# Numbers per token spread over partitions by DMAs through DRAM, rows scaled on GpSimd, and a new order of work

## What is computed

```python
def rmsnorm(x, gamma):
    n = jnp.linalg.norm(x, axis=-1, keepdims=True)
    return x / jnp.maximum(n, 1e-12) * SCALE * gamma
xn = rmsnorm(x, norm_gamma)                      # x here: the layer-normed rows, xn2 in the kernel
sn = rmsnorm(slot_embeds, slot_norm_gamma)       # 8 experts x 64 slots
logits = jnp.einsum('bnd,esd->bnes', xn, sn)
dispatch = jax.nn.softmax(logits, axis=1)        # over the tokens
combine = jax.nn.softmax(logits.reshape(b, n, e * s), axis=-1)   # over the slots, for each token
slots = jnp.einsum('bnd,bnes->besd', xn, dispatch)
h = gelu(jnp.einsum('besd,edh->besh', slots, w1) + b1)
eo = jnp.einsum('besh,ehd->besd', h, w2) + b2
out = jnp.einsum('bmd,bnm->bnd', eo, combine)
```

## Time and profile before

| | before |
|---|---|
| median of 3 runs | 1098.13 us (1097.9 to 1098.71) |
| profiled execution, its own time | 1098.24 us |
| its span (first to last instruction) | 1096.4 us, mean TensorE clock 0.992 of full speed |
| TensorE busy | 1062.8 us (97%) |
| VectorE busy | 960.2 us (88%) |
| ScalarE busy | 773.0 us (71%) |
| GpSimd busy | 606.9 us (55%) |
| share of the chain that ended last | PE 90%, DVE 6% |

### The profile page before, as it was taken

How to read it: one execution, slowest core, us unless ns; L and a number is a source line. 1 busy time by engine, 2 the same in 40 slices (tenths; PEclk the granted TensorE clock), 3 DMA queues, 4 the chain that set the end, 5 groups by cost and what they waited for, 6 DMA issues and landing times.

```text
span 1096.4 us, 27975 instructions
## 1 busy us (share of the span) xinstructions
PE 1062.8 (97%) x10436; PEld 832.9 (76%) x10436; DVE 960.2 (88%) x2074; ACT 773.0 (71%) x1450; POOL 606.9 (55%) x619
## 2 busy tenths in 40 slices
...
DMA packets 18468, 16.97 MB, mean 15 GB/s; under 512 B 800, under 2 KB 17440, under 8 KB 18080
## 3 DMA queue, kind: packets, MB, share of 16 engines
...
## 4 chain that ended last, share of the span: by engine, by line
PE 90%; DVE 6%; issue 1%; ACT 1%; POOL 0%; POOLq 0%; DVEq 0%; ACTq 0%
PE bank L1008 12%; PE bank L959 11%; PE bank L969 10%; PE bank_s L990 7%; PE bank L950 5%; PE bank L979 5%; PE bank L920 5%; PE bank L913 5%; PE bank L1035 3%; DVE ret L661 3%; PE bank L908 3%; PE bank L823 3%; PE bank L874 3%; PE bank L1018 3%; PE bank_s L993 2%; PE bank L854 2%
## 5 line engine op out<-in xcount | busy, mean ns | idle before, releaser
L329 POOL TENSOR_TENSOR ret_abs<-ret_abs 128x512 f32<-128x512 f32 x128 | 168.7, 1318 | 238.2 <-ACT ret_abs L485 238.2
L661 DVE TENSOR_TENSOR ret<-bank_s,k_sb 128x1536 f32<-128x1536 f32 x128 | 223.9, 1749 | 23.7 <-PE bank L1008 14.8
L334 POOL TENSOR_TENSOR urs<-uvar,mhalf 128x16 f32<-128x16 f32 x64 | 185.3, 2903 | 91.8 <-DVE uvar L677 91.8
L485 ACT ACTIVATE ret_abs<-ret 128x1536 f32<-128x1536 f32 x128 | 189.6, 1481 | 8.8 <-DVE ret L661 8.8
L959 PE MATMUL bank<-slotsT,w_sb 128*128 128x128 f32 x1024 | 140.9, 281 | 0.3 <-DVE hact L726 0.3
L969 PEld LDWEIGHTS bank<-w_sb,hact 128*128 128x128 f32 x1024 | 125.5, 192 | 14.7 <-issue 13.9
L969 PE MATMUL bank<-w_sb,hact 128*128 128x128 f32 x1024 | 134.1, 277 | 0.0
L959 PEld LDWEIGHTS bank<-slotsT,w_sb 128*128 128x128 f32 x1024 | 124.3, 192 | 10.3 <-issue 7.4
L340 POOL TENSOR_SCALAR dT<-dT,drec 128x256 f32<-128x256 f32 x128 | 83.4, 665 | 48.6 <-DVE drec L721 48.4
L1008 PE MATMUL bank<-ret,vrow 128*32 128x256 f32 (+1 forms) x2048 | 108.6, 329 | 0.3 <-DVE hact L726 0.2
L990 PE MATMUL bank_s<-qT,km 32*128 32x256 f32 x1024 | 91.4, 426 | 5.0 <-DVE ret L661 5.0
...
## 6 DMA issues: line engine op xcount, KB each, us to landing
x_sb<-x SPq DMA_DIRECT2D x16, 256.0 KB, 2.8
...
out<-attn SPq DMA_DIRECT2D x16, 256.0 KB, 2.3
...
slot_sb<-slot_rows SPq DMA_DIRECT2D x1, 256.0 KB, 3.5
```

Source lines behind the costliest of these rows:

```text
L329: pool.tensor_tensor(both[:, :, P:SEQ], both[:, :, P:SEQ], both[:, :, SEQ:3 * P], ALU.add)\
L334: pool.tensor_tensor(urs[:, j], uvar[:, j], mhalf[:], ALU.pow).then_inc(ready["urs"].sem, 1)
L485: act.activation(ret_abs[:, q % MR], ret[:, q % MR], ACT.Abs).then_inc(ready["ab"].sem, 1)
L661: dve.tensor_tensor(ret[:, q % MR], bank_s[:, :, 0:3 * P], causal.unsqueeze(1).broadcast_to([P, Q, 3 * P]), ALU.mult)\
```

## The change

The turned xn3 is no longer made by TensorE and ScalarE. SP writes `rnorm` (128 partitions x 4 numbers) to a DRAM row of 512 numbers, `turn[0]`, waits for it, and reads that row back to all 128 partitions as `fB`. GpSimd then multiplies the turned xn2 with `fB` (`xn3Tc`). In the same way `rmax` goes through `turn[1]` into `rB`, without TensorE and ScalarE. The row-wise xn3 stays, for `slots`, which now waits for it; the constant factor moves into rnorm. Removed are the tasks xn3T and rB on TensorE and xn3Tc and rBc on ScalarE; added are one GpSimd instruction and four DMAs a pair, on SP's queue, which gets a table of its own. All tables and the banks are new: xn2T, xn2 and rstd2/rnorm now stand in the next step (age 1), and h 6 and 7, eo 4 to 7, row 2 and 3, out and z one step later than before (age 2).

```diff
@@ -48,60 +48,59 @@
 ORDER = {
-    "PE": [("qk", 0, 1), ("xn3T", 0, 1), ("qk", 1, 1), ("vg", 0, 1), ("LT", 0, 1), ("LT", 1, 1), ("quad", 0, 1),
...
+    "PE": [("gatedT", 0, 2), ("eo", 4, 2), ("h", 6, 2), ("eo", 5, 2), ("xn2T", 0, 1), ("h", 7, 2), ("row", 2, 2),
...
+    "POOL": [("rstd2", 0, 1), ("rnorm", 0, 1), ("rstd", 0, 0), ("km", 0, 1), ("xn3Tc", 0, 1), ("urs", 2, 2),
...
+    "SP": [("load", 0, 0), ("fput", 0, 1), ("fget", 0, 1), ("store", 0, 3), ("mput", 0, 1), ("rBc", 0, 1)],
...
@@ -240,14 +242,39 @@
 
         @block.sync
         def _(sp):
-            def load_x(p):
+            def load(p, par=0, k=0):
+                since(sp, ready["x1"], p - 1)
                 sp.dma_start(x_sb[:], x[bass.ds(p * TOK, TOK), :].rearrange("(j p) c -> p j c", p=P)).then_inc(x_in.sem, 16)
 
-            def store(p):
+            def later_load(p, par, k):
+                if p:
+                    load(p)
+
+            def store(p, par, k):
                 sp.wait_ge(*ready["x2"](p))
                 sp.dma_start(out[bass.ds(p * TOK, TOK), :].rearrange("(j p) c -> p j c", p=P), attn[:]).then_inc(stored.sem, 16)
 
-            load_x(0)
+            def fput(p, par, k):
+                sp.wait_ge(*ready["rnorm"](p))
+                since(sp, got, p - 1)
+                sp.dma_start(turn[0].rearrange("(j p) -> p j", p=P), rnorm[:], allow_slow_non_contiguous=True).then_inc(put.sem, 16)
+
+            def fget(p, par, k):
+                sp.wait_ge(*put(p))
+                since(sp, ready["xn3Tc"], p - 1)
+                sp.dma_start(fB[:], turn[0].unsqueeze(0).broadcast_to([P, TOK])).then_inc(got.sem, 16)
+
+            def mput(p, par, k):
+                sp.wait_ge(*ready["rmax"](p))
+                since(sp, max_got, p - 1)
+                sp.dma_start(turn[1].rearrange("(j p) -> p j", p=P), rmax[:], allow_slow_non_contiguous=True).then_inc(max_put.sem, 16)
+
+            def mget(p, par, k):
+                sp.wait_ge(*max_put(p))
+                since(sp, ready["cs"], p - 1, 3)
+                sp.dma_start(rB[:], turn[1].unsqueeze(0).broadcast_to([P, TOK])).then_inc(max_got.sem, 16)
+
+            load(0)
             late_k, late_w, late_v = K_COLS["qdecay"][0], W_COLS["q1"][0], V_COLS["b2"][0]
             sp.dma_start(k_sb[:, 0:late_k], consts[:, 0:late_k]).then_inc(early.sem, 16)
             sp.dma_start(v_sb[:, 0:late_v], vectors[:, 0:late_v]).then_inc(early.sem, 16)
@@ -260,14 +287,7 @@
...
 
-            sp.wait_ge(*ready["x1"](0))
-            load_x(1)
-            for p in range(pairs - 2):
-                sp.wait_ge(*ready["x1"](p + 1))
-                load_x(p + 2)
-                store(p)
-            store(pairs - 2)
-            store(pairs - 1)
+            steps_of({"load": later_load, "store": store, "fput": fput, "fget": fget, "mput": mput, "rBc": mget}, ORDER["SP"])
             sp.wait_ge(*stored(pairs - 1))
 
         @block.gpsimd
@@ -311,9 +331,17 @@
                 pool.tensor_tensor(rn[:, 1], rn[:, 0], mv2[:, :, 1], ALU.mult).then_inc(ready["rn"].sem, 1)
                 pool.wait_ge(*ready["rn"](p, 1))
                 pool.sem_inc(passed["gpsimd"].sem, 1)
-                pool.tensor_scalar(rn[:, 2], rn[:, 1], float(C), 1e-24, ALU.mult, ALU.max).then_inc(ready["rn"].sem, 1)
+
+                pool.tensor_scalar(rn[:, 2], rn[:, 1], 1.0, 1e-24 / C, ALU.mult, ALU.max).then_inc(ready["rn"].sem, 1)
                 pool.wait_ge(*ready["rn"](p, 2))
+                since(pool, put, p - 1)
                 pool.tensor_tensor(rnorm[:], rn[:, 2], mhalf[:, 0:TILES], ALU.pow).then_inc(ready["rnorm"].sem, 1)
+
+            def xn3Tc(p, par, k):
+                pool.wait_ge(*got(p))
+                pool.wait_ge(*ready["xn2Tc"](p))
+                since(pool, filled["LT"], p - 1, 3)
+                pool.tensor_tensor(xn3T[:], xn2T[:].rearrange("p b n -> p (b n)"), fB[:], ALU.mult).then_inc(ready["xn3Tc"].sem, 1)
 
             def km_(p, par, q):
                 b, i = divmod(q, Q)
@@ -350,7 +378,7 @@
                 pool.wait_ge(ready["slot_rn"].sem, 1)
                 pool.tensor_tensor(slot_n[:, 2], slot_n[:, 1], mhalf[:, 0:4], ALU.pow).then_inc(ready["slot_rn"].sem, 1)
 
-            steps_of({"rstd": rstd_, "mixa": mixa, "rstd2": rstd2_, "rnorm": rnorm_, "km": km_,
+            steps_of({"rstd": rstd_, "mixa": mixa, "rstd2": rstd2_, "rnorm": rnorm_, "xn3Tc": xn3Tc, "km": km_,
                             "add": add, "urs": urs_, "dn": dn}, ORDER["POOL"],
                      between={("rstd", 0): derived, ("mixa", 0): slot_norms})
 
@@ -431,24 +459,15 @@
             def xn2Tc(p, par, k):
                 bank = bank_of("xn2T", p)
                 since(act, filled["vg"], p - 1, 3)
+                since(act, ready["xn3Tc"], p - 1)
                 since(act, filled["qk"], p - 1, 1)
                 act.activation(xn2T[:], bank[:].rearrange("p (b n) -> p b n", b=2), ACT.Copy)\
                     .then_inc(ready["xn2Tc"].sem, 1)
-
-            def xn3Tc(p, par, k):
-                bank = bank_of("xn3T", p)
-                since(act, filled["LT"], p - 1, 3)
-                act.activation(xn3T[:], bank[:], ACT.Copy).then_inc(ready["xn3Tc"].sem, 1)
 
             def LTc(p, par, m):
                 bank = bank_of("LT", p, m)
                 since(act, filled["out"], p - 1, 1)
                 act.activation(cT[:, m], bank[:], ACT.Copy).then_inc(ready["LTc"].sem, 1)
-
-            def rBc(p, par, k):
-                bank = bank_of("rB", p)
-                since(act, ready["cs"], p - 1, 3)
-                act.activation(rB[:], bank[:], ACT.Copy).then_inc(ready["rBc"].sem, 1)
 
             def ce(p, par, m):
                 act.wait_ge(*ready["cs"](p, m))
@@ -634,7 +653,7 @@
                 dve.wait_ge(*ready["xn2"](p))
                 since(dve, filled["slots"], p - 1, 1)
                 for j in range(TILES):
-                    ins = dve.tensor_scalar(xn3[:, j], xn2[:, j], rnorm[:, j:j + 1], C ** 0.5, ALU.mult, ALU.mult)
+                    ins = dve.tensor_scalar(xn3[:, j], xn2[:, j], rnorm[:, j:j + 1], 1.0, ALU.mult, ALU.mult)
                 ins.then_inc(ready["xn3"].sem, 1)
 
             def qkc(p, par, k):
@@ -706,12 +725,12 @@
 
             def rmax_(p, par, k):
                 bank = bank_of("mxT", p)
-                since(dve, filled["rB"], p - 1)
+                since(dve, max_put, p - 1)
                 dve.tensor_reduce(rmax[:], bank[:].rearrange("p (j s) -> p j s", j=TILES), X, ALU.max, negate=True)\
                    .then_inc(ready["rmax"].sem, 1)
 
             def cs(p, par, m):
-                dve.wait_ge(*ready["rBc"](p))
+                dve.wait_ge(*max_got(p))
                 dve.wait_ge(*ready["DTe"](p, m))
                 dve.wait_ge(*ready["mx"](p, 2))
                 dve.tensor_tensor(cT[:, m], cT[:, m], rB[:], ALU.add).then_inc(ready["cs"].sem, 1)
@@ -898,10 +917,6 @@
                 pe.wait_ge(*ready["xn2"](p))
                 turn_tiles(claim("xn2T", p), xn2, "xn2T")
 
-            def xn3T_(p, par, k):
-                pe.wait_ge(*ready["xn3"](p))
-                turn_tiles(claim("xn3T", p), xn3, "xn3T")
-
             def qk(p, par, k):
                 pe.wait_ge(*ready["xn2Tc"](p))
                 bank = claim("qk", p, k)
@@ -928,13 +943,6 @@
                     ins = pe.transpose(bank[:, j * P:(j + 1) * P], mx[:, j * P:(j + 1) * P], ident)
                 ins.then_inc(filled["mxT"].sem, 1)
 
-            def rB_(p, par, k):
-                pe.wait_ge(*ready["rmax"](p))
-                bank = claim("rB", p)
-                for j in range(TILES):
-                    ins = pe.transpose(bank[:, j * P:(j + 1) * P], rmax[:, j:j + 1].broadcast_to([P, P]), ident)
-                ins.then_inc(filled["rB"].sem, 1)
-
             def DT(p, par, m):
                 pe.wait_ge(*ready["dn"](p, m))
                 bank = claim("DT", p, m)
@@ -943,6 +951,7 @@
                 ins.then_inc(filled["DT"].sem, 1)
 
             def slots(p, par, b):
+                pe.wait_ge(*ready["xn3"](p))
                 pe.wait_ge(*ready["Dc"](p, 3))
                 bank = claim("slots", p, b)
                 for i in range(2):
@@ -1116,7 +1125,8 @@
     }
     nc = bacc.Bacc("TRN2", target_bir_lowering=False, num_devices=1)
     args = [nc.dram_tensor(n, u.shape, F32, kind="ExternalInput").ap() for n, u in arrays.items()]
+    turn = nc.dram_tensor("turn", [2, TOK], F32, kind="Internal").ap()
     out = nc.dram_tensor("out", arrays["x"].shape, F32, kind="ExternalOutput").ap()
-    build(nc, *args, out)
+    build(nc, *args, turn, out)
     r = run_bass_kernel_spmd(nc, [arrays], core_ids=[0])
     return r.results[0]["out"].reshape(x.shape)
```

74 lines of the change are left out of this document (39 added, 35 removed), and 34 rows, old and new, of tables (BANK, ORDER).

## The result

The changed kernel takes 1268.76 us (1267.93 to 1270.19, 4 runs) against 1098.02 before, a ratio of 1.1555 (95% interval 1.1535 to 1.1575). The prediction was 1089, with a range up to 1106: wrong in sign and by far in size.

A forecast was written before the change was run, and what follows sets the result against it. TensorE was taken to set the pace, VectorE having only 6 us of room. From the span of 1096.4: 14 steps -7.0, head -7.0, tail +4.1, 1086.5; plus 1.8 outside, 1088.3, taken as 1089 us; 8-in-10 range 1079 to 1106.

The forecast's parts named there:

- the loop through two steps: `local`, norm factor, DMAs, multiplication, GpSimd's queue, that pair's first `g` in the next step, then TensorE to the next `local`.
- The break-even of 5.9 us: DMAs between rnorm and GpSimd's multiplication stay hidden, by 0.5 us only, up to a round trip of 5.9 us.
- both roads to the first `g`: Counted from the start of `local`, TensorE arrives at `g` 0 at 29.2 us; GpSimd is ready at 28.7, or 29.6.
- The round trip: rnorm's write to DRAM and read back as fB: 2.3 + 2.8 + 0.3 for issues, 5.4 us; upper bound about 8.
- the third rival: Slow round trip: fB late, GpSimd's queue held and `g` 0 waits; 1111 us at a trip of 7.5; chance 0.25.
- The rate of one us a step: Each us of rnorm's round trip above 5.9 us makes the step one us longer.
- The DMAs of rmax are hidden by at least 7.5 us of work: VectorE's eleven pieces between rmax and the first `cs`, at least 7.5 us, cover a trip of some 5.4; costed at nothing.
- 64.74 us a step, plus 0.7 of waits: TensorE's step: 65.94 less 1.20 for transposes and a wait, plus waits of 0.4 at xn2T and 0.3 at slots: 65.45.
- four banks: Banks changing hands in under 2 us (out 1, vg 1, h 1, r 0), where an unforecast wait might appear.
- the second rival: Saving turns into small waits at xn2T, slots and changes from g to quad: 66.1 us a step, 1098 us; chance 0.20.
- Head and tail: First full step 58.4 us instead of 65.39, gaining 7.0; after the last `local` 86.4 against 82.3, losing 4.1.
- The rule of 512 B: The Trainium skill's smallest DMA transfer at line rate, below which the engine reads, modifies and writes; no price given.

## Why the prediction was wrong

- *What bounds the kernel, and the loop through two steps*: right. The stations of the loop were where they had been put: rnorm's write is issued 12.7 us after `local` (12.0 forecast), GpSimd's queue takes 9.86 us (9.9), and the first `g` follows the late multiplication. The break-even of 5.9 us for the round trip was nearly right as well, since a trip of 5.8 is hidden but for 0.35 us. That is in part luck: both roads to the first `g` are longer than forecast, TensorE's 31.1 us without the trips (29.2) and GpSimd's 30.8 with both writes in 16 B (28.7).
- *The round trip, 5.4 us with bounds up to 8*: the step that failed. It is 13.76 us: 8.57 for the write instead of 2.3 and 5.2 for the read instead of 2.8. The write was sized by the store's row, whose 512 pieces are as many but of 512 B each; the upper bound of 8 had no row behind it. The trip is 7.9 us above the break-even of 5.9; at the third rival's own rate, one us a step for each, that is 1089 + 14 x 7.9 = 1200, and some 1215 with head and tail. The mechanism was rival 3, which was priced up to a trip of 7.5.
- *The rate of one us a step*: nearly right, 6.8 to 7.6 us a step for a trip that is 8.0 to 8.4 longer. TensorE's lower clock, which no term had, does not seem to come on top. In the step shown it is low around the late `out`, while GpSimd's queue sets when `g` starts; from the first `g` to the next `local` it is full, 1.00. No run kept the clock up with the wait in place, so this is read from the order of events.

```profile
439.52:477.92 38.40, 36.46 (x387) 26.47 (x387) 33.22 (x59) 30.26 (x61) 20.67 (x20) 1.00 0.03 8
```

- *The DMAs of rmax are hidden by at least 7.5 us of work*: wrong through the same size. A trip of 13.5 us is longer than that, and costs 15 (1268.8 against 1253.8) to 25 us (1157.4 against 1132.3). The surplus falls between the first `g` and the next `local`: 38.4 us in the changed kernel, 37.1 with rmax's write in 16 B.
- *64.74 us a step, plus 0.7 of waits*: wrong too, and this alone would have turned the sign. Without trips the step is 67.94 us. Busy time is 65.51, and the waits are 2.41 us instead of 0.7: xn2T 0.67 (0.4 forecast), slots none (0.3), and two that the counting missed, xnT's bank 0.90 and DT 3 0.84. I named only four banks as places where a wait might appear, and did not work out xnT's; the second rival had small waits right in kind and at less than half of their size. With 14 steps of 68.00 instead of 65.45 the forecast of 1089 becomes 1125, and the run without trips has 1123.9.
- *Head and tail without trips*: right. 83.75 - 24.50 = 59.25 us (58.4 forecast) and 1122.2 - 1035.71 = 86.5 (86.4). With the trips they are 70.75 and 98.4, which is 23 us of the 146 that the trips add to the span; the 14 steps, at 76.76 instead of 68.00, are the other 123.
- *The store*: not priced. It stands behind the read of fB, lands in 5.4 us instead of 2.3, and `attn` and `out` wait for it. It is the first wait that the profile names, and the run with the store first shows that it isn't the one that sets the step.
- *The rule of 512 B*: the prediction gave it no price of its own. Pieces of 16 B are far below it and land in 1.4 us, so being below 512 B is not by itself what cost here.
